# Loading a graph-attention kernel's adjacency in 2 KB runs from both DMA queues, with parts of the setup moved to GpSimd

## The reference, cut to what matters

```
h = max(layernorm(x), 0)
Wh = h @ W;  f1 = Wh @ a1;  f2 = Wh @ a2
att = softmax(where(adj > 0, leaky_relu(f1 + f2.T, 0.2), -9e15))
x = x + relu(att @ Wh)
h = max(layernorm(x), 0)
node = h @ W1                                   # 8192 x 16
hw = einsum('nc,kcf->nkf', h, W2)
m = einsum('nk,nkf->nf', node, hw)
out = x + relu(adj @ m + node @ b)
```

## Time and profile before

| | us |
|---|---|
| median of 3 runs (lowest to highest) | 1750.87 (1746.13 to 1758.23) |
| span of the profiled execution | 1747.9 |
| PE busy | 1701.2 (97%) |
| DVE busy | 1290.1 (74%) |
| ACT busy | 1089.2 (62%) |
| POOL busy | 548.7 (31%) |

### The profile page before, as it was taken

How to read it: one execution, slowest core, us unless ns; L and a number is a source line. 1 busy time by engine, 2 the same in 40 slices (tenths; PEclk the granted TensorE clock), 3 DMA queues, 4 the chain that set the end, 5 groups by cost and what they waited for, 6 DMA issues and landing times.

```text
span 1747.9 us, 35898 instructions
## 1 busy us (share of the span) xinstructions
PE 1701.2 (97%) x11311; PEld 1468.8 (84%) x11311; DVE 1290.1 (74%) x1775; ACT 1089.2 (62%) x1889; POOL 548.7 (31%) x522
## 2 busy tenths in 40 slices
PE   8889899999999999999999999999999999999998
PEld 5789788888888988988888888898777788888886
DVE  8679688888888898888888888888566443533534
ACT  5554466767666677676676767663655655555554
POOL 0000044454453544544445445355444200000000
PEclk9999999999999999999999999999999999999999
DMA  9999999999999999999999999987533345453430
GB/s 236 280 347 367 324 279 315 298 328 303 292 321 310 300 315 307 306 303 313 311 295 312 320 291 315 311 245 288 208 140 145 122 171 193 154 204 144 168 144 24
DMA packets 316753, 452.23 MB, mean 259 GB/s; under 512 B 21072, under 2 KB 291616, under 8 KB 298912
## 3 DMA queue, kind: packets, MB, share of 16 engines
q1 hardware_dynamic: 164928, 228.63, 44.2%
q10 hardware_dynamic: 144944, 203.58, 39.0%
q0 software_dynamic: 6832, 19.41, 3.4%
HBM read 364.46 MB, written 87.07 MB: 258 GB/s over the span
## 4 chain that ended last, share of the span: by engine, by line
PE 81%; DMA 5%; SPq 4%; DVE 3%; issue 2%; ACTq 2%; ACT 1%; POOL 1%; DVEq 0%; POOLq 0%
PE ot_ps L820 42%; PE ot_ps L877 13%; PE mt_ps L877 13%; PE hw_ps L789 12%; SPq L295 3%; DMA maskT_d<-mt 2%; ACTq L295 2%; DMA xt<-in_x_dram 1%; ACT wh_mask L529 1%; DMA adj_sb<-in_adj_dram 1%; PE h_ps L784 1%; SPq L310 1%; DVE att L985 1%; DVE p_sb L1009 1%; POOL prod L406 1%
## 5 line engine op out<-in xcount | busy, mean ns | idle before, releaser
L820 PEld LDWEIGHTS ot_ps<-wh_mask,p_sb 128*128 128x128 f32 x8192 | 945.7, 193 | 84.6 <-issue 69.8
L820 PE MATMUL ot_ps<-wh_mask,p_sb 128*128 (+1 forms) x8192 | 954.7, 277 | 25.6 <-DVE p_sb L1009 20.7
L1009 DVE SCALAR_TENSOR_TENSOR p_sb<-zb,qcol,mt 128x1024 f32<-128x1024 uint8 (+1 forms) x512 | 729.7, 1442 | 17.9 <-DVE mt L933 10.0
L529 ACT ACTIVATE wh_mask<-adj_sb 128x2048 uint8<-128x2048 f32 x256 | 485.2, 1921 | 70.3 <-issue 53.4
L406 POOL TENSOR_TENSOR prod<-prod 128x1024 f32<-128x1024 f32 (+2 forms) x192 | 333.8, 1739 | 567.8 <-ACT prod L595 550.6
L1057 DVE CAST mask<-adj_sb 128x1024 fp32r<-128x1024 uint8 x272 | 204.0, 757 | 244.9 <-PE mt_ps L877 243.2
L622 ACT ACTIVATE mask<-adj_sb 128x1024 fp32r<-128x1024 uint8 x240 | 255.2, 1064 | 173.8 <-PE ot_ps L877 173.6
L595 ACT ACTIVATE prod<-hw_ps,node 128x128 f32<-128x128 f32 x1024 | 278.7, 383 | 113.2 <-PE hw_ps L789 111.7
L877 PE MATMUL mt_ps<-mask,msgs 128*128 128x512 f32 x1024 | 282.6, 398 | 2.1 <-DVE mask L1057 1.1
L877 PE MATMUL ot_ps<-mask,msgs 128*128 128x512 f32 x1024 | 274.7, 390 | 1.1 <-DVE mask L1057 0.5
L789 PE MATMUL hw_ps<-wcat,hT 128*128 128x512 f32 x512 | 240.7, 592 | 0.0
(11 more groups left out here) (108 smaller groups left out, 575.4 us busy)
## 6 DMA issues: line engine op xcount, KB each, us to landing
adj_sb<-in_adj_dram SPq DMA_DIRECT2D x536, 256.0 KB, 7.7
adj_sb<-in_adj_dram ACTq DMA_DIRECT2D x488, 256.0 KB, 8.9
maskT_d<-mt ACTq DMA_DIRECT2D x64, 1024.0 KB, 10.3
adj_sb<-maskT_d SPq DMA_DIRECT2D x32, 2048.0 KB, 7.7
keep_d<-keep POOLq DMA_DIRECT2D x64, 128.0 KB, 6.0
p_sb<-keep_d SPq DMA_DIRECT2D x4, 2048.0 KB, 12.0
msg_d<-msg POOLq DMA_DIRECT2D x56, 128.0 KB, 5.8
msgs<-msg_d SPq DMA_DIRECT2D x7, 1024.0 KB, 9.0
```

What stands on the lines that cost most here:

```text
L529: ins = act.activation(m8[:, q // 2, 2 * (q % 2) + part, :], adj_sb[:, q, part * T * COLS:(part + 1) * T * COLS], ACT.Copy, scale=EDGE)
L820: ins = pe.matmul(ot_ps[h][:, (t - t0) * ROW:(t - t0 + 1) * ROW], p_sb[:, r, t * P:(t + 1) * P], rows, start=begin and t == t0, stop=end a ...
L1009: dve.scalar_tensor_tensor(p_sb[:, r, :], zbf[:, bass.ds((ib % 2) * BLK, BLK)], qcol[:, bass.ds(tile + b_, 1)], mtb[:, p, k // 2, :, 2 * ( ...
```

## The change

- **Runs of 2 KB.** A buffer of `adj_sb` now belongs to a group c of 32 x 8 rows and holds all 2048 columns of a turn, both halves h; a DMA moves 512 KB in runs of 512 columns (2 KB). Per turn there are 16 such DMAs instead of 32 of 256 KB. Which rows of the matrix make up a block changes with it (`group(ib, c)`), so `x`, `xt` and the output are moved in 4 pieces of 32 partitions each.
- **Both queues from the start.** ACT starts with its 8 loads of the first turn; SP sends `x` (32 DMAs of 128 KB), then its 8 loads of the first turn. W2 is loaded behind SP's turns 1 to 3 instead of behind turn 0. The five small parameters go from ACT's queue to POOL's.
- **GpSimd in the setup.** POOL normalizes 3 of the 8 tiles of every block, makes 4 of the 8 first casts, and copies the first block of `x` to `xt`, so that block's `xt` is not loaded.
- **First z.** PE multiplies a matrix whose columns repeat W a1 with h of the first block (L813), f1 in every partition; DVE adds and clips it, ACT takes its exponential. The diagonal matrix is gone.
- **Order on ACT.** Casts go by (c, h); the tile sums are copied before the last loads of the first block are issued; `xt` is loaded by SP. The later W2 wait stands behind the first block.

```diff
-        def load_quadrants(eng, ib, jg, p, h, quadrants):
-            q = 2 * p + h
-            for part in range(2):
-                for a in quadrants:
-                    eng.dma_start(adj_sb[a * SQ:(a + 1) * SQ, q, part * T * COLS:(part + 1) * T * COLS]
...
+        def load_quadrants(eng, ib, jg, c, quadrants):
+            for a in quadrants:
+                eng.dma_start(adj_sb[a * SQ:(a + 1) * SQ, c, :].rearrange("r (t n) -> r t n", n=2 * COLS),
+                              adj_v[bass.ds(group(ib, c), 1), :, :, bass.ds(jg * 2 * BLK + a * 2 * COLS, 2 * COLS)]
+                              .rearrange("g r t n -> (g r) t n")).then_inc(adj_in[c], 16)
@@ sync
+            def load_x(i):
+                for c in range(A):
+                    sp.dma_start(wh[c * SQ:(c + 1) * SQ, i * T:(i + 1) * T, :], x_v[group(i, c)])\
+                      .then_inc(x_in[i], 16)
             for i in range(NB):
-                sp.dma_start(wh[:, i * T:(i + 1) * T, :], x_v[i]).then_inc(x_in[i], 16)
-            for h in range(2):
-                load_adj(0, 0, 0, h)
+                load_x(i)
+            for c in range(A):
+                load_quadrants(sp, 0, 0, c, (0, 1))
...
@@ gpsimd
+            pool.sem_inc(xt_in, 16 * A - 1)
+            pool.wait_ge(x_in[0], 16 * A)
+            pool.tensor_copy(xt[:, :, :], wh[:, 0:T, :]).then_inc(xt_in, 1)
+
+            def norm(i):
+                pool.wait_ge(rstd8_done, i + 1)
...
+                for t in range(PART, T):
...
+            def cast(c, h):
+                pool.wait_ge(adj_in[c], 16 * A)
+                pool.tensor_scalar(m8[:, h, c, :].rearrange("p (t n) -> p t n", n=COLS), adj_halves[:, c, :, h, :],
+                                   EDGE, None, ALU.mult).then_inc(adj_cast[h][c], 1)
+
+            norm(0)
...
+            for i in range(1, NB):
+                norm(i)
+                if i >= NB - 3:
+                    cast(*((0, 0), (0, 1), (1, 0))[i - NB + 3])
+            cast(1, 1)
@@ scalar
+            for c in range(A):
+                load_quadrants(act, 0, 0, c, (2, 3))
...
+            load_upper(1, 0)
+            load_upper(1, 1)
             cast(2, 1, 1, 0)
+            load_upper(1, 2)
+            cast(3, 1, 1, 0)
             act.activation(std[:, :], eps[:, :], ACT.Sqrt)
...
-                        if ends_block(jg) and p == 1 and k == 3:
+                        if ends and k == 3:
                             if last:
                                 convert(0, True, 0)
                             copy_sums(ib)
-                        ahead = None if last else lambda: cast(2 * p, 1, i + 2, A * n + A)
+                            if sums_wait:
+                                load_upper(i + 2, 2 * p)
+                        ahead = None if last else lambda: cast(2 * p + 1, 0, i + 2, 2 * A * i + 2 * p + 2)
...
-                        if k == 1 and not last:
-                            cast(2 * p, 0, i + 2, A * n + A)
+                        if k < 2 and not last:
+                            cast(2 * p, k, i + 2, A * (2 * i + k) + 2 * p + 1)
                         if k == (3 if sums_wait else 2) and not last:
-                            cast(2 * p + 1, 0, i + 2, A * n + A)
+                            cast(2 * p + 1, 1, i + 2, A * (2 * i + 1) + 2 * p + 2)
@@ vector
-                            if k % 2 == 0:
-                                dve.wait_ge(adj_cast[2 * (1 - p) + k // 2], i + 1 + p)
+                            dve.wait_ge(adj_cast[1 - p][k], i + 1 + p)
```

More of the change, by code:

```diff
@@ L55, in build, with group @@
     COLS = BLK // A
-    adj_v = adj.rearrange("(i c r t) n -> i c r t n", c=A, r=SQ, t=T)
-    x_v = x.rearrange("(i p t) f -> i p t f", p=P, t=T)
-    out_v = out.rearrange("(i p t) f -> i p t f", p=P, t=T)
+    GR = SQ * T
+    adj_v = adj.rearrange("(g r t) n -> g r t n", r=SQ, t=T)
+    x_v = x.rearrange("(g r t) f -> g r t f", r=SQ, t=T)
+    out_v = out.rearrange("(g r t) f -> g r t f", r=SQ, t=T)
+    assert GR == COLS and IT * 2 * A == N // GR
+    def group(ib, c):
+        return ib // 2 * (2 * A) + ib % 2 + 2 * c
     zrow_d = nc.dram_tensor("zrow_d", [NT, P], FP32).ap()
@@ new lines, in load_xt, with turn @@
+            def load_xt(pb):
+                sp.wait_ge(mv_done, T * pb + 1)
+                for c in range(A):
+                    sp.dma_start(xt[c * SQ:(c + 1) * SQ, :, :], x_v[bass.ds(group(pb, c), 1)]
+                                 .rearrange("g r t f -> (g r) t f")).then_inc(xt_in, 16)
+            for i in range(NB):
+                load_x(i)
+            for c in range(A):
+                load_quadrants(sp, 0, 0, c, (0, 1))
+            def turn(i, ib, jg, rows=False):
+                for c in range(A):
+                    sp.wait_ge(adj_cast[1][c], i)
+                    load_quadrants(sp, ib, jg, c, (0, 1))
+                    if rows and c == 2:
+                        load_xt(ib - 1)
@@ L313, in _, with turns @@
+            def turns(ib, first, rows=False):
+                for jg in range(first, IT):
+                    turn(ib * IT + jg, ib, jg, rows and jg == 1)
+            turns(0, 1)
             sp.dma_start(wcat[:, 0:K * D].rearrange("c (k f) -> c k f", f=D),
                          W2.rearrange("k c f -> c k f")).then_inc(w2_in, 16)
-            def turn(i, ib, jg, finish, last):
-                for p in range(2):
-                    for h in range(2):
-                        q = 2 * p + h
-                        if not (isinstance(i, int) and i == 0 and p == 0):
-                            sp.wait_ge(adj_cast[q], i)
-                            load_adj(ib, jg, p, h)
@@ L324, in _ @@
-            attention_loop(sp, turn, loads=True)
-            for q in range(4):
-                sp.wait_ge(adj_cast[q], NB * IT)
+            turns(1, 0)
+            with sp.Fori(0, NB - 2) as before:
+                turns(before + 2, 0, True)
+            load_xt(NB - 1)
+            for c in range(A):
+                sp.wait_ge(adj_cast[1][c], NB * IT)
             for p in range(2):
@@ L769, in _ @@
               .then_inc(setup_pe, 1)
-            idle_run(9)
-            for h in range(2):
-                pe.wait_ge(diag_done, h + 1)
-                pe.matmul(hw_ps[h][:, :], ones[:, :], zdiag[:, 4 * h:4 * h + 4, :].rearrange("p t f -> p (t f)"),
-                          start=True, stop=True).then_inc(z0_done, 1)
+            idle_run(6, mt_ps[0])
+            pe.wait_ge(setup_act, 7)
             pe.wait_ge(setup_dve, 13)
@@ L919, in norm @@
                     dve.wait_ge(xnT_done, 2 * (i - 1))
-                for t in range(T):
+                for t in range(PART):
                     n = T * i + t
@@ L923, in norm @@
                                             ALU.subtract, ALU.mult)
-                ins.then_inc(xn8_done, 1)
+                    if t >= 3:
+                        ins.then_inc(xn8_done, 1)
             statistics(0)
-            for i in range(NB):
+            norm(0)
+            statistics(1)
+            for i in range(1, NB):
                 if i + 1 < NB:
@@ L969, in scale_rows @@
                                   ALU.mult).then_inc(wh_scaled, 1)
-            dve.wait_ge(setup_act, 7)
+            dve.wait_ge(setup_dve, 11)
+            dve.wait_ge(setup_act, 5)
             dve.tensor_copy(whx[:, :, D], bcol[:, :]).then_inc(wh_scaled, 1)
             scale_rows(0)
+            dve.tensor_reduce(hsum1[:, :], hsum[:, :], AX.X, ALU.add).then_inc(setup_dve, 1)
+            dve.wait_ge(setup_dve, 12)
+            dve.tensor_scalar(hrep[:, :], ones[:, :], hsum1[:, :], None, ALU.mult).then_inc(setup_dve, 1)
+            for c in range(2, A):
+                first_squares(c)
             def finish_tile(k, p, u, m, t, pb):
```

171 lines of the change are left out of this document (89 added, 82 removed).

## The result

| | before | after |
|---|---|---|
| median (lowest to highest), 4 runs each | 1748.5 (1743.15 to 1758.23) | 1771.64 (1770.66 to 1772.91) |
| span of the profiled execution | 1747.9 | 1769.3 |
| PE busy | 1701.2 | 1698.2 |
| POOL busy | 548.7 | 700.6 |

The ratio is 1.0125, 95% interval 1.0085 to 1.0165. I forecast 1739, 1726 to 1754. Some executions of the kernel before lie in a disturbed state, at 1768 to 1795 us; all comparisons leave them out.

A forecast was written before the change was run, and what follows sets the result against it. PE's own work was taken to bound 339 to 1210 us and the gather, with gains only before 207 us, where DVE paces the setup. Terms +4 - 9 - 8 + 1 = -12: span 1735.9, median 1739 us, range 1726 to 1754.

The forecast's parts named there:

- Arrival of x, a loss: Setup: adj on ACT's queue shares the DMA engines, so x's second block lands at 20 us, its statistics ending about 22.2.
- GpSimd beside DVE: Setup: POOL's normalizations and casts hold up DVE or come late themselves, 3 us together; last normalization at 49.8.
- The lock, my second rival: Setup: POOL's normalizations and casts hold DVE for all their time, 12.4 and 6.2 us; median 1753, chance 0.13.
- From the last normalization to PE's start: End of the setup: a shorter chain gains 1.6 us; PE starts at 65.2, 4 us later than before.
- The first block, a gain: First attention block: adj has more lead, one wait of 3 us remains and the others go, -9 us.
- Block boundary and xt, a gain: End of first block, start of second: earlier copy of the sums and no xt wait, -8 us in all.
- The rest: Remaining parts, mainly the gather's end: three more store issues of about 0.36 us, +1 us.
- Wide runs themselves are no term: adj loads: packet size does not set the transfer rate, so wider runs add nothing to the sum.
- The rule that the prediction set against it: Trainium skill: DMAs under 2 KB have significant overhead each; by it the first block's whole 13 us would go.
- Rival 4: Every turn: group 3's cast comes too late, 1.2 us lost in each of 28 later turns; 1773, chance 0.07.

The follow-up runs named there:

- f1: The changed kernel with SP's last xt load behind the first messages and POOL's four casts on ACT: 1756.86 us, ratio 1.0035.
- e3: The changed kernel with only POOL's four casts given back to ACT: 1766.85 us, ratio 1.0102.
- g1: f2 with the first turn's adj loads alone in 1 KB runs, all left halves first: 1745.56 us, ratio 0.9965.
- g2: g1 with the first store of the mask ahead of all six loads of the second turn: 1742.59 us, ratio 0.9951.
- e1: The changed kernel with only SP's last load of xt put behind the masks and first messages: 1760.61 us, ratio 1.0041.
- f2: f1 with all 16 first loads of adj on SP's queue behind x, none on ACT's: 1756.11 us, ratio 1.0016.
- f3: f1 with every load of adj split in two of 1 KB runs, in all turns: 1779.78 us, ratio 1.0156.

## Why the prediction was wrong

PE's start was forecast at 65.2 us and measured at 84.75. The 19.5 us between them are 8.2 for x (the second statistics end at 30.43 instead of 22.2), 8.6 for POOL (its last normalization ends 36.2 us behind that, where the sum had 24.6 and 3), and 2.7 for the chain behind it (18.1 us instead of 15.4).

- **"Arrival of x, a loss"** had the mechanism right (turns by packets: 496 to 496) and the size wrong. I divided by 300 GB/s; the mix ran at 220, and the second block was there at 28.11 instead of 20. x alone in pieces of 32 partitions came at 197 to 206 GB/s, not at the 296 of the earlier trace rows: I took a rate of one form of DMA for another, and so it was with adj (217 GB/s in its new form against 249). About +8 us.
- **"GpSimd beside DVE"**, 3 us, failed in the part on the casts. The last normalization came 11.6 us later than without any cost of POOL, where I had 3. The casts took 5.37 us each, above my bound of 4.8, and POOL needed 18.1 us for its normalizations of the last three blocks and the two casts between, where I had 10.2 to 15.0. The lock, my second rival, held for the casts and DVE's normalizations, 3.6 us; it didn't for POOL's normalizations, for which I had the 12.4 us. With the casts gone (f1) the last normalization is 27.8 us behind the second statistics, just the 24.6 and 3, so the 3 us paid for the split alone and nothing was there for the casts. Left out altogether was who waits for them behind that: DVE's second transpose, 12.43 us, and a small operation in the start's chain, 3.41. e3 puts the casts at 10.3 us together.
- **"From the last normalization to PE's start"**, a gain of 1.6, did not come. It is 17.3 us in e3, f1 and g1, where no cast of POOL stands in it, against 17.0 before. Nor did the sum ask what PE does in it: with the diagonal product gone PE has next to nothing to do there, its clock falls, and the first 160 matmuls cost 2.3 us more. No run gave PE more zeros there.
- **What the first half turn needs** was no step at all. I counted adj's bytes as lead for the first block, and not that a 2 KB run doubles what must land before it, 8.4 MB for 4.2. It was hidden behind the terms above in the changed kernel; g1 put it at 14.8 us once they were gone.
- **"The first block, a gain"** and **"Block boundary and xt, a gain"** came as forecast, 16.0 us for 17. But g1 and g2 show what the first block's gain was: adj had a lead because the start was late. With the start at 58 the block took 132.6, as before, 2.4 of it for the clock at the start. Setup and first block together, the time to the first sums, were 194.2 before, 207.8 after, 190.2 in g2.
- **"The rest", +1**, missed 12.6 us. The sum put xt's move from ACT's queue to SP's at nothing for the gather, without a reason. I followed xt to the start of the second block, and not the last one, which on SP stands ahead of the masks and messages. e1 shows it: 12.0 us.
- **"Wide runs themselves are no term"**: true of the rate (217 GB/s in 2 KB runs in f2, 218 in 1 KB runs in g1). The rule that the prediction set against it speaks of whole DMAs, and the smallest here has 128 KB. But the number of issues is a term: with each load in two DMAs, blocks two to eight take 20.7 us more (f3), and ACT waits for its own issuing.
- Rival 4, the late cast of group 3, did not come: PE was busy for 864.27 us of 871 against 867.25.

## What to carry to other kernels

Before widening a load, count what must land before the first consumer can start: a wider run brings bytes that only a later step needs, and the first turn may want the narrow form where the loop wants the wide one. A gain in one stretch that rests on data being early is paid by the stretch before it; judge both by one landmark behind them. Follow every moved transfer to its last instance, and look at what stands behind it in its queue.
